# One gather tile in 64 of a graph layer's second loop: fetched row by row on SyncE instead of gathered on GpSimd

## The chip, the cores and the metric

One core of one Trainium2 chip. The metric is the device time of one execution in microseconds. The runs of the kernel before took 2174.53, 2178.26 and 2182.04 us; the median is 2178.26 us.

## What is computed

Two layers of a graph network, on 6,250 nodes (128 numbers each) and 106,250 edges that are sorted by receiving node. The first layer is finished when the stretch of this case begins. The second layer, cut to what matters:

```python
src, dst = edge_index
msg_in = concat([x[src], x[dst]], axis=1)            # 106250 x 256
for t in range(4):                                    # four edge types
    h = relu(msg_in @ W1[t] + b1[t]);  m = h @ W2[t] + b2[t]
    score = sigmoid(msg_in @ attn_w[t] + attn_b[t])
    msgs += where(edge_type == t, m * score, 0)
agg = zeros.at[dst].add(msgs)
x = layernorm(layernorm(gru(agg, x) + x) * gamma + beta + x)   # per node
```

`x[src] @ W1` does not depend on the edge but on the pair (node, type). The kernel therefore makes a table of it first, `p_tab` in DRAM, with one row of 129 f32 numbers (516 bytes) for each node and type: 128 for the hidden layer and one for the score. For each edge one row of that table has to be fetched, by a row number that is data.

## The kernel before, in words

Two loops over the edges stand one behind the other, one for each layer; the change lies in the second (function `edges1`). Edges are cut into tiles of 128 (one edge on each partition), 8 tiles make a step (`TPS`), and 4 steps make a loop (`SLOTS`), one for each slot of the ring buffer `gp[:, slot, tile, :]`. There are 104 steps (`STEPS`) in 26 loops (`LOOPS`), 831 tiles in all, since the last step has 7.

**GpSimd (POOL)** does the gathers. `gather_step` (L636) issues one indirect DMA for each tile (L639): it takes 128 row numbers from the index tile `idx` and fetches 128 rows of `p_tab` into `gp`. `gather_loop` (L645) runs the steps: before each it waits for the index tile (`idx_in`), for the slot to be free (`used`, one count for each step whose rows were added by VectorE), and from loop `LEAD_LONG` = 6 on for `paced` (`e_mm`, TensorE's count of finished groups), which holds GpSimd back to at most two steps ahead of TensorE.

**VectorE (DVE)**, in `edge_rows` (L2175), waits for a slot's gathers (`landed[u]`, 16 for each tile) and adds the gathered rows to TensorE's receiver rows: three additions for a step (L2187). It then frees the slot (`used`), adds sums into the accumulators (L2164, L2167) and makes one-hot matrices (L2142 to L2150). **ScalarE (ACT)** applies sigmoid and relu (L1886, L1890), and its queue also issues the index tiles (`load_idx`, L1762), the receivers' windows (`load_windows`, L1754, four DMAs for a step whose row numbers are loaded into registers by `run_starts`, L632 and L633) and the key rows (`load_row`). **TensorE (PE)** multiplies the windows by one-hot matrices (L2005) and sums the messages (L2094).

Behind the edges run the nodes, in units of 256: unit g = i - 3 is worked on in loop i, a piece in each of the four steps. Its transfers are all that **SyncE (SP)** does in this stretch, in the loop at L1840: wait for `xt_used`, load `x_t` (L1824, read by TensorE in `node_gates`, first at L2028, and by VectorE); wait for `y_ok` in `store` (L1829) and write the previous unit's rows to `out` (L1831, waited for in VectorE's `new_rows`, L2305); wait for `xr_used` and load the rows `x_row` (L1827). The order on each engine's queue is written out by hand, and all waits are on semaphores.

Of the kernel before, what the change touches and what calls it, by code (L numbers as in the profile page):

```python
# [23 lines left out]
P = 128  # L24
# [38 lines left out]
N_LATER = 29  # L63
FULL = -(-E // P) - (STEPS - 1) * TPS
FIRST_PART = 4
KEY_AT = 2 * TPS * P + PPS
ROWS = -(-(STEPS + 2) // 16) * 16

# [48 lines left out]
def build(nc, a, out):  # L117

    top = ExitStack()
    with top:  # L120
# [22 lines left out]
            x1=nc.dram_tensor("x1_d", [NP, H], f32).ap(),  # L143
            x1_t=nc.dram_tensor("x1_t_d", [P, CHUNKS * CH * P], f32).ap(),
            p_tab=nc.dram_tensor("p_tab_d", [NP * T, PW], f32).ap(),
            q_tab=nc.dram_tensor("q_tab_d", [CHUNKS * CH * P * T, PW], f32).ap(),
        )
        later = update_weights(nc, m)
# [493 lines left out]
        ).then_inc(landed[h], 16)  # L642


def gather_loop(e, idx, idx_in, table, buf, landed, used, gate, last_landed, paced, rate):  # L645


    slots = len(landed)

    def steps(start, stop, pace):  # L650
        with e.Fori(start, stop) as i:  # L651
            for h in range(slots):
                e.wait_ge(idx_in[h], i * 16 + 16)
                e.sem_inc(gate, 1)
                e.wait_ge(used, i * slots + (h + 1))  # L655
                e.sem_inc(gate, 1)  # L656
                if pace:
                    e.wait_ge(paced, i * (slots * rate) + rate * (h + 1 - LEAD))  # L658
                    e.sem_inc(gate, 1)
                gather_step(e, idx, table, buf, landed, h)  # L660

    steps(1, LEAD_LONG, False)
    steps(LEAD_LONG, LOOPS - 1, True)
    for h in range(slots):
        e.wait_ge(idx_in[h], (LOOPS - 1) * 16 + 16)
        e.sem_inc(gate, 1)
        e.wait_ge(used, (LOOPS - 1) * slots + (h + 1))
        e.sem_inc(gate, 1)
        e.wait_ge(paced, rate * ((LOOPS - 1) * slots + (h + 1 - LEAD)))
        e.sem_inc(gate, 1)  # L670
        if h < slots - 1:
            gather_step(e, idx, table, buf, landed, h)
    gather_step(e, idx, table, buf, landed, slots - 1, range(FIRST_PART))
    gather_step(e, idx, table, buf, dict([(slots - 1, last_landed)]), slots - 1, range(FIRST_PART, FULL))

# [995 lines left out]
def edges1(nc, k, dram, later, nodes, out, left):  # L1671


    with ExitStack() as ctx:
# [16 lines left out]
        ps_s = ps_row[:, 0:2 * PPS * WIN].rearrange("p (h g w) -> p h g w", h=2, g=PPS)  # L1691
        iota, part = ps_row[:, 2 * PPS * WIN:2 * PPS * WIN + P], ps_row[:, 3 * P:3 * P + 1]
        landed = m.sems("landed1", SLOTS)
        win_in, row_in = m.sems("win_in", 2), m.sems("row_in", 2)
        gate = gate_v = k["gate"]
        (used, hot_ok, hx_ok, e_mm, pre_ok, score_ok, hid_ok, sc_ok, sum_mm, acc_own, score_own, zero_ok) = (
# [49 lines left out]
        def own_count(g, z):  # L1746
            return 0 if z is last_rest else g

        def own_f_count(g, z):
            return own_count(g, z) * OWN_F - (1 if z is first_rest else 0)  # L1750

        with nc.Block(no_gpsimd_drain=True) as block:

# [12 lines left out]
            def _(e):  # L1766
# [70 lines left out]
                load_x_t(0, UN, usual)  # L1837
                e.wait_ge(xr_used, 1)
                load_x_row(0, UN, usual)
                with e.Fori(1, UNITS) as g:  # L1840
                    e.wait_ge(xt_used, g + 1)
                    load_x_t(g, UN, usual)
                    store(g - 1, UN, usual)
                    e.wait_ge(xr_used, g + 1)
                    load_x_row(g, UN, usual)
                for (g, n), z, u in zip(REST, (first_rest, last_rest), (1, 0)):
                    e.wait_ge(used, SLOTS + STEPS - SLOTS + u + 1)
                    e.wait_ge(xt_ld, 16 * g)
                    load_x_t(g, n, z)
# [12 lines left out]
            @block.gpsimd  # L1862
            def _(e):
                for u in range(SLOTS):
                    e.wait_ge(idx_in[u], 16)
                    e.sem_inc(gate, 1)
                    gather_step(e, idx, dram["p_tab"], gp, landed, u)
                gather_loop(e, idx, idx_in, dram["p_tab"], gp, landed, used, gate, landed[SLOTS - 1], e_mm, NQ)

                def root(g, n, c, z):  # L1870
                    mine = rstd[:, z["at"]:z["at"] + n // P]
                    e.wait_ge(z["var_ok"], own_count(g, z) * 2 + (c + 1))
                    e.tensor_tensor(mine, mine, minus_half[:, 0:n // P], ALU.pow).then_inc(z["root_ok"], 1)

                for c in range(2):
                    root(UNITS - 1, UN, c, before_rest)
                left.run(e, "gpsimd", left.flag(e, "gpsimd"))

            @block.scalar
            def _(e):  # L1880
# [54 lines left out]
                def steps(i, unit, before, first=False, last=False, table=False):  # L1935
                    for u in range(SLOTS):
                        j, h = i * SLOTS + u, u % 2
                        if not last and not first:
                            e.wait_ge(landed[u], i * (16 * TPS) + 16 * TPS)
                            load_idx(e, j + SLOTS, u)  # L1940
                        if table:
                            table_out(j + (AHEAD - 1), CH - 1)
# [196 lines left out]
            def _(e):  # L2139
# [32 lines left out]
                    some = slice(lo * CH, hi * CH)  # L2172
                    e.memset(first_buf[:, some, :], 0.0).then_inc(zero_ok, 1)

                def edge_rows(i, u, before, clear=False, final=False):  # L2175


                    j, h = i * SLOTS + u, u % 2
# [1 line left out]
                    if gone:  # L2180
                        e.memset(gp[:, u, FULL:TPS, :], 0.0).then_inc(iota_ok, 1)
                        e.wait_ge(iota_ok, 3)
                    e.wait_ge(landed[u], i * (16 * TPS) + 16 * (FULL if gone else TPS))
                    for q, mine in enumerate(groups):
                        n = mine.stop - mine.start
                        e.wait_ge(e_mm, j * NQ + (q + 1))
# [142 lines left out]
                def steps(i, first, unit, before, last=False):  # L2329
                    for u in range(SLOTS):  # L2330
                        if last and u == SLOTS - 1:
                            adds(STEPS - 2, 0)
                        edge_rows(i, u, not first or u > 0, first and u == 1, last)
                        if first and u == 0:
                            clear_first(0, CH)
                        if before and u == 0:
# [124 lines left out]
```

## Time and profile before

| what | value |
|---|---|
| runs of the kernel before | 2174.53, 2178.26, 2182.04 us |
| the profiled execution's own time | 2180.23 us |
| its span in the trace | 2178.1 us |
| second loop's gathers, first start to last start | 1107.63 to 2149.43 us |
| granted TensorE clock, mean of the span | 0.895 |

Times in the trace count from the first instruction. A queue's name with a q behind it (SPq, ACTq, POOLq) is the engine's own instruction stream: DMA issues, register arithmetic and semaphore instructions stand there and are not counted as busy. FUSED_REGOPS, ALU_OP and MOVE are register arithmetic, TENSOR_LOAD reads registers from memory. The duration of a DMA instruction is what its issue takes on the engine; the time until its data is there is called landing.

### The profile page before, as it was taken

How to read it: one execution, taken by the hardware profiler on the slowest of the kernel's cores; microseconds unless marked ns; L12 is line 12 of the kernel's file. 1: busy time of each engine (PE TensorE's matmuls, PEld its weight loads, DVE VectorE, ACT ScalarE, POOL GpSimd, SP SyncE). 2: the span in 40 equal slices, each digit the busy share in tenths (PEclk: the TensorE clock that was granted, in tenths of full speed). 3: DMA queues.
4: the chain of work that ended last, by engine and by line, in shares of the span. 5: the costliest groups of instructions: out<-in, count | busy, mean ns of one | idle time of the engine just before them, and what ended most of it. 6: DMA issues, size and time to landing. Idle time of an engine off the chain costs nothing. (4 is left out here: it accounts for less than half of the span.)

```text
span 2178.1 us, 43658 instructions
## 1 busy us (share of the span) xinstructions
PE 1773.3 (81%) x9981; PEld 1422.8 (65%) x9981; DVE 1470.1 (67%) x3717; ACT 1334.7 (61%) x4373; POOL 1606.5 (74%) x1698
## 2 busy tenths in 40 slices
PE   6897999999999999999877876766766666677767
PEld 3675766676666666666646775666666666666666
DVE  6657655555655555555557687777777777777877
ACT  6676877777877877777535544544554454544444
POOL 6777777777777777777657777777777777777773
PEclk7898999999999999999989988888887988887888
DMA  8422233232322322322368855454444445444452
GB/s 287 126 56 59 75 83 80 73 87 75 83 78 75 84 77 76 82 78 75 83 177 231 225 122 122 109 117 117 115 117 112 117 113 119 110 119 116 110 124 53
DMA packets 220027, 236.10 MB, mean 108 GB/s; under 512 B 72844, under 2 KB 162744, under 8 KB 219547
## 3 DMA queue, kind: packets, MB, share of 16 engines
q0 software_dynamic: 53744, 112.66, 22.1%
q10 hardware_dynamic: 87968, 56.13, 10.2%
q1 hardware_dynamic: 78267, 66.78, 9.9%
q8 instruction: 16, 0.26, 0.0%
q14 instruction: 32, 0.26, 0.0%
HBM read 190.83 MB, written 44.57 MB: 108 GB/s over the span
## 5 line engine op out<-in xcount | busy, mean ns | idle before, releaser
L639 POOL DMA_INDIRECT gp<-p_tab_d,idx x831 | 789.6, 950 | 277.7 <-issue 247.9
L639 POOL DMA_INDIRECT gx<-node_d,idx x831 | 800.2, 963 | 262.4 <-issue 235.7
L729 ACT ACTIVATE msg<-ws,y 128x32 f32<-128x32 f32 x2448 | 539.9, 309 | 86.2 <-DVE ws L705 85.8
L1000 PEld LDWEIGHTS ps_a<-hot,msg 128*128 128x128 f32 x3324 | 412.0, 199 | 209.0 <-DVE msg L714 106.5
L2005 PE MATMUL ps_e<-win,hot_x 128*128 128x129 f32 x1664 | 303.0, 356 | 266.2 <-DVE hid L2187 243.6
L1000 PE MATMUL ps_a<-hot,msg 128*128 128x128 f32 x3324 | 435.0, 286 | 75.8 <-DVE msg L714 53.5
L2005 PEld LDWEIGHTS ps_e<-win,hot_x 128*128 128x128 f32 x1664 | 278.5, 261 | 288.8 <-DVE hid L2187 250.8
L708 DVE TENSOR_TENSOR vy<-gx,y 128x768 f32<-128x768 f32 (+1 forms) x105 | 99.6, 948 | 307.6 <-DMA gx<-node_d,idx 307.5
L1890 ACT ACTIVATE hid<-hid,score 128x128 f32<-128x128 f32 x832 | 277.9, 393 | 10.1
L2187 DVE TENSOR_TENSOR hid<-ps_e,gp 128x387 f32<-128x387 f32 (+1 forms) x312 | 141.7, 509 | 143.2 <-DMA gp<-p_tab_d,idx 139.3
L1886 ACT ACTIVATE score<-hid 128x3 f32<-128x3 f32 (+1 forms) x312 | 61.0, 195 | 272.5 <-DVE hid L2187 267.8
L687 PE MATMUL ps_w<-w,h 128*128 128x256 f32 x832 | 223.4, 415 | 0.0
L2094 PEld LDWEIGHTS ps_g<-hot,hid 128*128 128x128 f32 x1664 | 212.1, 200 | 6.4 <-ACT hid L1890 0.3
L2094 PE MATMUL ps_g<-hot,hid 128*128 128x128 f32 x1664 | 212.0, 282 | 0.1
L687 PEld LDWEIGHTS ps_w<-w,h 128*128 128x128 f32 x832 | 159.3, 202 | 67.9 <-issue 48.3
L190 ACT ACTIVATE h<-ps_h,b 128x512 f32<-128x512 f32 x208 | 141.3, 679 | 85.2 <-PE ps_h L195 81.6
L2142 DVE TENSOR_TENSOR hot_x<-key_row,ps_s 128x1024 f32<-128x1024 bf16 x104 | 126.0, 1212 | 32.8 <-PE ps_s L2100 27.5
L2164 DVE TENSOR_TENSOR acc<-acc,ps_g 128x128 f32 x416 | 119.5, 287 | 14.4 <-issue 2.1
L1140 DVE TENSOR_TENSOR hot<-ps_a,dloc 128x1024 f32<-128x1024 f32 x104 | 126.6, 1217 | 0.0
L2150 DVE TENSOR_TENSOR hot<-ps_s,key 128x1024 f32<-128x1024 f32 x104 | 126.4, 1215 | 0.0
L996 PE MATMUL ps_h<-emb,w 16*128 16x512 f32 x202 | 113.2, 640 | 2.4 <-DMA emb<-emb_d 2.4
L195 PE MATMUL ps_h<-h,w 128*128 128x512 f32 x208 | 110.1, 611 | 0.7 <-ACT h L190 0.7
(295 smaller groups left out, 2155.2 us busy)
## 6 DMA issues: line engine op xcount, KB each, us to landing
win<-q_tab_d ACTq DMA_DIRECT2D x408, 64.5 KB
key_row<-key_row_d ACTq DMA_DIRECT2D x100, 256.0 KB, 3.9
gx<-node_d,idx POOLq DMA_INDIRECT x831, 2.7
gp<-p_tab_d,idx POOLq DMA_INDIRECT x831
p_tab_d<-acc SPq DMA_DIRECT2D x23, 516.0 KB
q_tab_d<-unit_area SPq DMA_DIRECT2D x36, 258.0 KB, 3.9
q_tab_d<-acc SPq DMA_DIRECT2D x5, 774.0 KB, 5.3
emb<-emb_d SPq DMA_DIRECT2D x102, 32.0 KB
```

The costliest lines, as they stand in the source:

```text
L190: e.activation(mlp[f"h{layer}"][:], mlp["ps_h"][:], ACT.Silu, bias=w[f"b{layer - 1}"][:]).then_inc(ok, 1)
L639: e.indirect_dma_start(out=buf[:, h, t, :], out_offset=None, in_=table, in_offset=bass.IndirectOffsetOnAxis(ap=idx[:, h, t:t + 1], axis=0) ...
L687: last = e.matmul(ps_w[:, 2 * t:2 * t + 2, :], h2[:, t * P:(t + 1) * P], w["w2"][:], start=False, stop=t % 2 == 1)
L729: last = e.activation(self.cols[1][:, tile, c, :], self.ws[:, tile, :], ACT.Copy, scale=y[:, c:c + 1])
L1000: last = e.matmul(ps_a[:, h, b, :], msgs[h].tile(t, b), hot[:, h, t, :], start=t == tiles.start, stop=t == tiles.stop - 1)
L1140: e.tensor_tensor(hot[:, h], spread(ps_a[:, h, IOTA, :], 1, TPS), spread(w["dloc"][:, bass.ds(j * TPS, TPS)], 2, P), ALU.is_equal)
L1890: last = e.activation(hid[:, h, t, 0:H], hid[:, h, t, 0:H], ACT.Relu, scale=score[:, h, t:t + 1])
L2005: last = e.matmul(ps_e[:, q, at:at + PW], hot_x[:, h, t, :], win[:, h, t // 2, :], start=True, stop=True)
L2094: e.matmul(ps_g[:, h, t // 2, :], hid[:, h, t, 0:H], hot[:, h, t, :], start=t % 2 == 0, stop=t % 2 == 1)
L2142: e.tensor_tensor(hot_x[:, h].rearrange("p t n -> p (t n)"), key_row[:, h, :], part.to_broadcast([P, TPS * P]), ALU.is_equal).then_inc(hx_ ...
L2150: e.tensor_tensor(hot[:, h], spread(iota[:, 0:P], 1, TPS), spread(k["key"][:, tiles], 2, P), ALU.is_equal).then_inc(hot_ok, 1)
L2187: e.tensor_tensor(hid[:, h, mine, :], ps_e[:, q, 0:n * PW].rearrange("p (t n) -> p t n", t=n), gp[:, u, mine, :], ALU.add).then_inc(pre_ok, 1)
```

## The change

The last tile of the last slot (slot 3, tile 7) is taken from GpSimd in every second loop from loop 6 on: loops 6, 8, ..., 24, which makes `FAR_TILES` = 10 tiles of the 831. In those loops GpSimd gathers 31 tiles and in the others 32, so its loop is written with two rounds in the body.

SyncE fetches these tiles. At its start it copies the ten columns of row numbers from `p_idx` into `far_idx` in DRAM with one DMA (10 x 128 numbers of 4 bytes, both sides non-contiguous). For each tile it loads the tile's 128 row numbers into one partition of `far_i`; then it loads 16 of them at a time into registers and issues 16 DMAs, each of one row of `p_tab` (516 bytes) into one partition of the side buffer `far[:, b, :]`, which has two halves and lies in the unused constant `zero`. Of the 128 rows 64 are issued in each of two loops: 48 between the load of `x_t` and the store, and 16 behind the load of `x_row`. When all 128 have landed (`far_ld`) and the ring's slot is free (`used`), one DMA copies the half into `gp[:, 3, 7, :]`.

The waits change with it: VectorE and ScalarE wait in slot 3 for a count of `landed` that leaves the moved tiles out (`last_landed`, register arithmetic on the loop's number), VectorE also for the copy (`far_ok`); a `sem_inc` of the unused count `gate` stands behind each of these waits, in ScalarE in all four slots.

```diff
 FIRST_PART = 4
+FAR_TILES = (LOOPS - LEAD_LONG) // 2
+FAR_REGS = 16
+FAR_EARLY = 48
 KEY_AT = 2 * TPS * P + PPS
...
             p_tab=nc.dram_tensor("p_tab_d", [NP * T, PW], f32).ap(),
+            far_idx=nc.dram_tensor("far_idx_d", [FAR_TILES, P], u32).ap(),
             q_tab=nc.dram_tensor("q_tab_d", [CHUNKS * CH * P * T, PW], f32).ap(),
...
 
-def gather_loop(e, idx, idx_in, table, buf, landed, used, gate, last_landed, paced, rate):
+def gather_loop(e, idx, idx_in, table, buf, landed, used, gate, last_landed, paced, rate, far=False):
 
...
 
-    def steps(start, stop, pace):
-        with e.Fori(start, stop) as i:
-            for h in range(slots):
-                e.wait_ge(idx_in[h], i * 16 + 16)
+    def round_of(i, pace, tiles=TPS):
+        for h in range(slots):
+            e.wait_ge(idx_in[h], i * 16 + 16)
+            e.sem_inc(gate, 1)
+            e.wait_ge(used, i * slots + (h + 1))
+            e.sem_inc(gate, 1)
+            if pace:
+                e.wait_ge(paced, i * (slots * rate) + rate * (h + 1 - LEAD))
                 e.sem_inc(gate, 1)
-                e.wait_ge(used, i * slots + (h + 1))
-                e.sem_inc(gate, 1)
-                if pace:
-                    e.wait_ge(paced, i * (slots * rate) + rate * (h + 1 - LEAD))
-                    e.sem_inc(gate, 1)
-                gather_step(e, idx, table, buf, landed, h)
-
-    steps(1, LEAD_LONG, False)
-    steps(LEAD_LONG, LOOPS - 1, True)
+            gather_step(e, idx, table, buf, landed, h, range(tiles if h == slots - 1 else TPS))
+
+    with e.Fori(1, LEAD_LONG) as i:
+        round_of(i, False)
+    if far:
+        with e.Fori(0, FAR_TILES - 1) as q:
+            round_of(q * 2 + LEAD_LONG, True, TPS - 1)
+            round_of(q * 2 + (LEAD_LONG + 1), True)
+        round_of(LEAD_LONG + 2 * (FAR_TILES - 1), True, TPS - 1)
+    else:
+        with e.Fori(LEAD_LONG, LOOPS - 1) as i:
+            round_of(i, True)
     for h in range(slots):
...
         landed = m.sems("landed1", SLOTS)
+        far = k["zero"][:, 0:2 * PW].rearrange("p (b f) -> p b f", b=2)
+        far_i = k["zero"][0:1, 2 * PW:2 * PW + P].bitcast(u32)
+        far_in, far_ok, far_ld = m.sem("far_in"), m.sem("far_ok"), m.sems("far_ld", 2)
         win_in, row_in = m.sems("win_in", 2), m.sems("row_in", 2)
...
 
+        def last_landed(i, n=TPS):
+            if isinstance(i, int):
+                return i * (16 * TPS) + 16 * n - 16 * max(0, (i - (LEAD_LONG - 2)) // 2)
+            pair = (i - (LEAD_LONG - 2)) // 2
+            return pair * (16 * (2 * TPS - 1)) + (i % 2) * (16 * TPS) + 16 * TPS * (LEAD_LONG - 1)
+
+        def far_count(i):
+            if isinstance(i, int):
+                return 16 * max(0, (i - (LEAD_LONG - 2)) // 2) + 32
+            return (i - (LEAD_LONG - 2)) // 2 * 16 + 32
+
         with nc.Block(no_gpsimd_drain=True) as block:
...
                 load_x_row(0, UN, usual)
-                with e.Fori(1, UNITS) as g:
+                first_far = (LEAD_LONG + 1) * SLOTS * TPS - 1
+                far_cols = dram["p_idx"][:, first_far:first_far + (FAR_TILES - 1) * 2 * SLOTS * TPS + 1:2 * SLOTS * TPS]
+                e.dma_start(dram["far_idx"].rearrange("q p -> p q"), far_cols, allow_slow_non_contiguous=True)\
+                    .then_inc(far_in, 16)
+                e.wait_ge(far_in, 16)
+                e.sem_inc(far_ok, 32)
+                far_regs = [e.alloc_register(f"far{n}") for n in range(FAR_REGS)]
+
+                def far_rows(b, lo, hi):
+                    for at in range(lo, hi, FAR_REGS):
+                        e.load(far_regs, far_i[:, at:at + FAR_REGS])
+                        for n, r in enumerate(far_regs):
+                            row = e.snap(r, min_val=0, max_val=NP * T - 1)
+                            e.dma_start(far[at + n:at + n + 1, b, :], dram["p_tab"][bass.ds(row, 1), :])\
+                                .then_inc(far_ld[b], 16)
+
+                def unit_io(g, rows=None):
                     e.wait_ge(xt_used, g + 1)
                     load_x_t(g, UN, usual)
+                    if rows is not None:
+                        b, lo = rows
+                        far_rows(b, lo, lo + FAR_EARLY)
                     store(g - 1, UN, usual)
...
                     load_x_row(g, UN, usual)
+                    if rows is not None:
+                        far_rows(b, lo + FAR_EARLY, lo + P // 2)
+
+                with e.Fori(0, FAR_TILES // 2) as n:
+                    for b in range(2):
+                        at, g = n * 4 + (2 * b + LEAD_LONG), n * 4 + (2 * b + 1)
+                        e.dma_start(far_i, dram["far_idx"][bass.ds(n * 2 + b, 1), :]).then_inc(far_in, 16)
+                        e.wait_ge(far_ok, n * 32 + (16 * b + 16))
+                        e.sem_inc(gate, 1)
+                        e.wait_ge(far_in, n * 32 + (16 * b + 32))
+                        e.sem_inc(gate, 1)
+                        unit_io(g, (b, 0))
+                        unit_io(g + 1, (b, P // 2))
+                        e.wait_ge(far_ld[b], n * (16 * P) + 16 * P)
+                        e.sem_inc(gate, 1)
+                        e.wait_ge(used, at * SLOTS + SLOTS)
+                        e.sem_inc(gate, 1)
+                        e.dma_start(gp[:, SLOTS - 1, TPS - 1, :], far[:, b, :]).then_inc(far_ok, 16)
+                with e.Fori(2 * FAR_TILES + 1, UNITS) as g:
+                    unit_io(g)
                 for (g, n), z, u in zip(REST, (first_rest, last_rest), (1, 0)):
...
                     gather_step(e, idx, dram["p_tab"], gp, landed, u)
-                gather_loop(e, idx, idx_in, dram["p_tab"], gp, landed, used, gate, landed[SLOTS - 1], e_mm, NQ)
+                gather_loop(e, idx, idx_in, dram["p_tab"], gp, landed, used, gate, landed[SLOTS - 1], e_mm, NQ, far=True)
 
...
                         if not last and not first:
-                            e.wait_ge(landed[u], i * (16 * TPS) + 16 * TPS)
+                            if u == SLOTS - 1 and unit:
+                                e.wait_ge(landed[u], last_landed(i))
+                            else:
+                                e.wait_ge(landed[u], i * (16 * TPS) + 16 * TPS)
+                            e.sem_inc(gate, 1)
                             load_idx(e, j + SLOTS, u)
...
 
-                def edge_rows(i, u, before, clear=False, final=False):
+                def edge_rows(i, u, unit, before, clear=False, final=False):
 
...
                         e.wait_ge(iota_ok, 3)
-                    e.wait_ge(landed[u], i * (16 * TPS) + 16 * (FULL if gone else TPS))
+                    if u == SLOTS - 1 and unit:
+                        e.wait_ge(landed[u], last_landed(i, FULL if gone else TPS))
+                        e.sem_inc(gate, 1)
+                        e.wait_ge(far_ok, far_count(i))
+                        e.sem_inc(gate, 1)
+                    else:
+                        e.wait_ge(landed[u], i * (16 * TPS) + 16 * TPS)
                     for q, mine in enumerate(groups):
...
                             adds(STEPS - 2, 0)
-                        edge_rows(i, u, not first or u > 0, first and u == 1, last)
+                        edge_rows(i, u, unit, not first or u > 0, first and u == 1, last)
                         if first and u == 0:
```

## Rows read from the trace of the kernel before

**Rows 1.** Page, part 1, busy time of the engines over the whole span.

```profile
PE 1773.3 (81%) x9981; PEld 1422.8 (65%) x9981; DVE 1470.1 (67%) x3717; ACT 1334.7 (61%) x4373; POOL 1606.5 (74%) x1698
```

**Rows 2.** Page, part 4, the chain that ended last, shares by engine.

```profile
POOL 30%; issue 13%; PE 2%; DMA 2%; DVE 1%; POOLq 0%; ACT 0%; DVEq 0%
```

**Rows 3.** Page, part 5, gathers of the second loop: busy, mean ns, idle.

```profile
L639 POOL DMA_INDIRECT gp<-p_tab_d,idx x831 | 789.6, 950 | 277.7 <-issue 247.9
```

**Rows 4.** Who waited for whom, POOL, 1100 to 2178 us.

```profile
POOL gp L639 <- issue: 247.9, 813, 0.3
POOL gp L639 <- PE ps_e L2005: 4.6, 15, 0.3
```

**Rows 5.** Timeline of POOL: first and last of the 831 gathers.

```profile
1107.63 0.94 POOL L639 DMA_INDIRECT gp<-p_tab_d,idx  x1 [24.58 <-POOLq L783]
...
2149.43 0.94 POOL L639 DMA_INDIRECT gp<-p_tab_d,idx  x1 [0.30 <-issue]
```

**Rows 6.** Timeline of one loop: two of SP's transfers, PE's use of x_t.

```profile
1710.66 0.40 SPq L1831 DMA_DIRECT2D out<-unit_area  x1
...
1719.05 0.34 SPq L1824 DMA_DIRECT2D unit_area<-x_t_d  x1
...
1734.74 0.60 PE L2028 MATMUL ps_v<-unit_area,w_ih 128*128 128x256 f32 x2
...
1759.35 0.34 SPq L1824 DMA_DIRECT2D unit_area<-x_t_d  x1
```

**Rows 7.** Stretch 1400 to 2100 us: busy time, clock, DMA share, GB/s.

```profile
1400.00:2100.00 700.00, 489.57 (x2930) 454.86 (x2931) 544.91 (x1637) 341.43 (x944) 530.16 (x558) 0.83 0.49 115
```

**Rows 8.** Timeline of DVE, the step's first addition, slots 2, 3, 0.

```profile
1701.93 1.36 DVE L2187 TENSOR_TENSOR hid<-ps_e,gp 128x387 f32<-128x387 f32 x3 [0.52 <-DMA gp<-p_tab_d,idx]
...
1711.94 1.36 DVE L2187 TENSOR_TENSOR hid<-ps_e,gp 128x387 f32<-128x387 f32 x3 [1.47 <-DMA gp<-p_tab_d,idx]
...
1722.46 1.36 DVE L2187 TENSOR_TENSOR hid<-ps_e,gp 128x387 f32<-128x387 f32 x3 [2.71 <-DMA gp<-p_tab_d,idx]
```

**Rows 9.** Line L1756 (window DMAs with row numbers in registers), by operation.

```profile
L1756 ACTq MOVE win<-q_tab_d x408: 29/29/29, 1143.0 to 2138.6; - x136
L1756 ACTq DMA_DIRECT2D win<-q_tab_d x408: 339/340/1064, 1143.1 to 2138.7; - x136
L1756 ACTq FUSED_REGOPS  x306: 46/46/57, 1143.5 to 2138.5; - x153
```

**Rows 10.** Timeline: four such DMAs in a row on ACT.

```profile
1705.73 1.86 ACTq L1756 DMA_DIRECT2D win<-q_tab_d  x4
```

**Rows 11.** Line L264, small loads of 4 rows and of 3 rows.

```profile
L264 SPq DMA_DIRECT2D b<-in_b x4: 297/330/413, 83.0 to 84.1; - x4
L264 SPq DMA_DIRECT2D att_b<-in_attn_b x1: 276/276/276, 78.1 to 78.1; - x1
```

**Rows 12.** Timeline: four loads of 4 rows each, one after another, on SP.

```profile
82.99 1.50 SPq L264 DMA_DIRECT2D b<-in_b  x4
```

**Rows 13.** Lines L1145 (one register loaded), L632 (four) and L633 (their snaps).

```profile
L1145 DVEq TENSOR_LOAD <-start x105: 302/308/1019, 71.8 to 1095.3; - x105
...
L632 DVEq TENSOR_LOAD <-start x104: 339/344/362, 1151.4 to 2159.8; - x104
L632 ACTq TENSOR_LOAD <-start x102: 303/308/729, 1142.5 to 2136.6; - x102
...
L633 ACTq FUSED_REGOPS  x102: 163/163/170, 1142.8 to 2136.9; - x102
```

**Rows 14.** Lines L1824 and L1831, transfers of 128 KB: issue to landing.

```profile
DMA to landing us min/median/max: 1.8/3.1/3.4
...
DMA to landing us min/median/max: 1.7/2.1/2.6
```

**Rows 15.** Page, part 3, queues that fetch instructions: packets, MB, share.

```profile
q8 instruction: 16, 0.26, 0.0%
q14 instruction: 32, 0.26, 0.0%
```

## The prediction, made before the changed kernel ran

> **What bounds the kernel now.** The page comes first. Over the whole span POOL is busy 74%, less than PE's 81% and little more than DVE's 67% [rows 1]; by these shares nothing would be decided. But they mix two loops and the work around them, and the chain that ended last is made of POOL for 30% and of "issue" for 13%, against 2% for PE and 1% for DVE [rows 2]. The costliest group says what that is: 831 gathers of 950 ns, with 0.3 us of idle time in front of each that ends with no release, only with the next issue [rows 3]. So one gather costs POOL 1.25 us from start to start whatever else happens. The list of waits from 1100 us on confirms it: 813 gaps of at most 0.3 us have no release, 15 of the same length are put down to PE, and there is no longer one in the loop [rows 4]. The first gather starts at 1107.63 us and the last at 2149.43 us: 1041.80 us over 830 intervals are 1.2552 us for each [rows 5]. The loop is 831 gathers long and nothing else. A loop of 32 tiles takes 40.17 us, and SP's timeline has that rhythm too: its loads of x_t start at 1719.05 and 1759.35 us [rows 6].
>
> The engines behind POOL have room. From 1400 to 2100 us DVE is busy 545 of 700 us, PE 490 and ACT 341 [rows 7]. DVE's first addition of a step waits for the gathers' landing every time: 0.52 us in slot 2, 1.47 in slot 3, 2.71 in slot 0 [rows 8].
>
> **The change, part by part.** The removed part: ten gathers less on POOL, 10 x 1.2552 = 12.6 us, all on the path that sets the end, since the last moved tile (loop 24) lies before the last gather and the tail behind it stays as it is. POOL's extra register arithmetic for the unrolled rounds costs nothing: its stream runs ahead of gathers of 1.25 us, and every gap is 0.3 us in the loop that has such arithmetic today [rows 4]. If that cover failed, a step's few operations of 0.03 to 0.06 us would show as longer gaps.
>
> What follows in the far step: slot 3's gathers are issued in 8.76 instead of 10.04 us, so they land 1.26 us earlier against DVE's work. DVE's idle time there is 1.47 us [rows 8], less some ten added queue operations (arithmetic of `last_landed` and `far_count`, two counts, one more wait), at the 46 ns of a FUSED_REGOPS [rows 9] about 0.4 us. DVE may be 0.2 us late in ten steps; the next slot has 2.71 us of room, and POOL does not notice, as it waits for `used` and `paced` only of steps it passed long ago. Cost: nothing; without that room, 10 x 0.2 = 2 us at most. ScalarE's added counts (four in a loop) and its own arithmetic lie beside its idle half [rows 7].
>
> The added part is SP's, and the question is whether SP gets 128 rows, 8 register loads and its old work done within two loops, 2 x 40.17 - 1.26 = 79.1 us. There is no such one-row DMA in the trace. Its nearest relatives:
> - With row numbers in registers, ACT issues four window DMAs in 1.86 us; one takes 0.34 us, so from start to start it is (1.86 - 0.34) / 3 = 0.507 us [rows 10], of which 0.340 is the DMA and 0.167 the MOVE, the FUSED_REGOPS and the gaps [rows 9]. These have 128 rows.
> - Loads of 4 rows or 3 rows take 276 to 330 ns, one 413 [rows 11], and four of them in a row 1.50 us, 0.375 each with a gap [rows 12]. I take 0.30 us for the DMA itself.
> - Each row is also snapped; four snaps and the first address take ACT 163 ns [rows 13], so about 0.035 us for one if it is merged into the address operation.
> I take 0.30 + 0.167 + 0.035 = 0.50 us for a row. Below, 0.276 + 0.121 = 0.40 (no gap lengthened); above, 0.507 + 0.046 = 0.553 (the row costs what the 128-row DMA costs, and its snap is an operation of its own).
> - Loading one register takes DVE 308 ns, four 344; ACT loads four in 308 [rows 13]. The slope is 12 ns a register: 16 cost 0.31 + 12 x 0.012 = 0.45 us, with a gap 0.50. Upper end by rows: each register for itself, 4.9 us.
> - Six old transfers at 0.47 us: 2.8 us. The copy and the fetch of row numbers 0.9 us; two waits for landing (row numbers, last rows), as a 128 KB transfer lands in 2.1 us [rows 14], 4.2 us.
> - SP's loop body has some 800 instructions, and its backward jump may wait for code. The whole run shows 48 packets of instruction fetch [rows 15], so before most loops never fetch; I put 0 to 3.4 us (the longest landing of rows 14) on each pass of four loops, and take 1 us for two loops.
>
> Sum for two loops: 128 x 0.50 = 64.3 (with 0.502), 8 x 0.50 = 4.0, 2.8, 0.9, 4.2 and 1.0: 77.2 of 79.1 us. It fits, with 2 us to spare. The order fits as well: 48 rows take 24 us and three loads 1.5, so they end 26 us behind the load of x_t, while the store's release comes 31.8 us behind it (1710.66 + 40.17 - 1719.05) [rows 6]; the last 16 rows then run about 1 us into the next x_t, and the end of a pair makes that about 6 us. PE needs x_t 15.7 us behind its load (1734.74 - 1719.05) [rows 6], of which landing takes 3.4 at most [rows 14]: 12.3 us may be lost before anybody waits. The finished side buffer is due one loop behind its copy, 40 us, and costs nothing. The DMA that collects the ten columns runs once, in front of SP's loop; if it takes long, it spends some of these 12.3 us once.
>
> SP's rows also load the DMA engines. 128 rows of 516 bytes replace 128 gathered rows, and the copy moves them once more; at a share of 0.49 [rows 7] that delays a landing by some tenths at most, not POOL's issue.
>
> On register loads the rows and a rule differ. The Trainium skill, page "Runtime: NRT & Kernel Launch", section "Instruction fetch mechanics", says that a register load costs about 200 ns a register even in bulk; it speaks of loads from HBM, ours read SBUF, and the 12 ns a register above speak against it here. By the page 16 registers would take 3.2 us and SP 99.2 us for two loops. That is a rival below, and its time is worked out there from rows.
>
> The sum: the profiled execution took 2180.23 us (span 2178.1), 2 us above the median of the runs. 2180.2 - 12.6 = 2167.7 us for it, 2178.3 - 12.6 = 2165.7 us against the median. I forecast **2166 us**.
>
> **The rivals.**
> A. The forecast: POOL stays the bound. Chance 0.61.
> B. SP becomes the bound, and the kernel gets slower. Its place is PE's wait for x_t in `node_gates`; behind it stand the receivers' products of the next step, so DVE, and through `paced` POOL. It decides from the point where two loops on SP exceed 79.1 us by more than 12.3/10 us, that is from 0.527 us for a row. At 0.553 us SP needs 128 x 0.553 + 12.9 = 83.7 us; 10 x 4.6 - 12.3 = 34 us are lost, 12.6 won: 2178 + 21 = 2199 us. For it: one-row DMAs may cost as much as large ones, and ACT's 0.507 us [rows 10] is close to the limit. Against: the small loads' 0.28 to 0.33 us [rows 11]. Chance 0.20.
> C. Registers load one after the other: by rows, 16 x 0.308 = 4.9 us instead of 0.45, SP 77.2 + 8 x 4.48 = 113 us for two loops, 10 x 33.9 - 12.3 - 12.6 = 314 us more: 2492 us. The Trainium skill's 200 ns would give 2178 + 10 x 20.1 - 24.9 = 2354 us (an estimate from the page named above). The 12 ns a register speak against both. Chance 0.04.
> D. Half-way: SP late by just as much as was won, a row at 0.53 to 0.542 us, or a code fetch at each jump at its upper end: between 2170 and 2185 us. Chance 0.13.
> E. The gathers' issue slows down because SP's row stream keeps DMA engines busy. Against: over the whole loop, with all the transfers it has today, the mean is 1.2552 us and no gap is long [rows 4, 5]. Chance 0.02, about 2180 us.
>
> **How the numbers follow.** About 0.3%, 6.5 us, is what a measurement of this kernel can tell from no change. Faster by more than that is A and little else: 0.62. Within it lie most of D and E: 0.13. Slower: B, C and the rest of D: 0.25. The range runs from 2161 us (the sum, less the 4 us by which the fastest run before lay under its median) to 2200 us, which takes in D and B's worked case and leaves C and the worse half of B out.
>
> **What would show it.** Right: 821 gathers on POOL, still 1.25 us apart with gaps of 0.3 us, the last starting near 2137 us; on SP one-row DMAs 0.50 us apart, register loads under 0.5 us, the store issued within 1 us of its release; DVE's idle time in slot 3 of far steps near 0.2 us and still ended by a landing. Wrong: PE L2028 waiting for unit_area<-x_t_d, or POOL gaps ended by PE L2005 that exceed 0.3 us (B); TENSOR_LOAD of some microseconds (C); idle time of SP in front of the DMA behind a jump (D); a mean gather above 1.26 us (E).

## The result, and the profile after

The changed kernel takes 2290.66 us (median of 5 runs, 2283.91 to 2292.39), the kernel before beside it 2182.04 us: ratio 1.0496, 95% interval 1.0481 to 1.0511, 108.6 us slower. Beside e1 to e4 below the kernel before itself took 2842 us and beside e5 to e7 2812 us, and the traces of those seven kernels have added gaps of about 3 us in front of 33 to 48 gathers, so that mainly the durations of single instructions are read from them, and the runs that decide stand beside a kernel before of 2176 to 2180 us.

Page of the changed kernel, part 1; it answers to [rows 1].

```profile
PE 1778.8 (78%) x9981; PEld 1420.0 (62%) x9981; DVE 1469.4 (64%) x3717; ACT 1330.5 (58%) x4373; POOL 1600.8 (70%) x1688
```

POOL's busy time is 5.7 us less, and the other engines' is what it was; nothing in the row says why the span grew by 108.6 us. Part 4 of the same page does (the chain that ended last, by engine and then by line), where [rows 2] had POOL 30%:

```profile
SPq 31%; issue 10%; DMA 3%; PE 2%; DVE 2%; POOL 1%; ACT 1%; ACTq 1%; DVEq 0%; POOLq 0%
SPq L1878 14%; SPq L1875 12%; SPq L1877 2%; POOL gp L643 1%; DMA win<-q_tab_d 1%; PE ps_e L2073 1%; DMA zero<-p_tab_d 1%; DMA zero<-far_idx_d 1%; DMA q_tab_d<-unit_area 1%; ACT hid L1954 1%; ACTq L1781 0%; SPq L1852 0%; SPq L1856 0%; PE ps_g L2162 0%; SPq L1849 0%
```

SP's instruction stream is now the chain: L1878 is the one-row DMA, L1875 the load of 16 registers, and L1877 the snap. Part 5 (busy, mean ns of one, idle before), beside [rows 3]:

```profile
L643 POOL DMA_INDIRECT gp<-p_tab_d,idx x821 | 781.1, 951 | 383.3 <-issue 236.2
L2096 PE MATMUL ps_v<-unit_area,w_ih 128*128 128x256 f32 x96 | 49.3, 613 | 153.6 <-DMA unit_area<-x_t_d 153.6
```

A gather is what it was, 951 ns, and there are ten less. The idle time in front of them grew from 277.7 to 383.3 us. The second row is new among the costliest groups: TensorE waits 153.6 us for x_t, the load of SP that stands behind the rows. Who waited for whom, POOL's waits first (us in total, times, longest), beside [rows 4], then the other engines' from 1350 to 2250 us:

```profile
POOL gp L643 <- issue: 236.2, 772, 0.6
POOL gp L643 <- PE ps_e L2073: 120.1, 42, 10.7
```

```profile
PE ps_v L2096 <- DMA unit_area<-x_t_d: 153.6, 19, 12.4
DVE unit_area L2382 <- DMA out<-unit_area: 81.8, 18, 5.8
```

POOL is held back by `paced` in 42 places, up to 10.7 us long, where before the 15 gaps put down to PE were 0.3 us each. 120.1 - 42 x 0.3 = 107.5 us were lost so. TensorE waits 19 times for x_t, about 8 us each, and VectorE's wait at L2382 for the store of `out` (another of SP's transfers) is new too. Timeline of POOL, first and last gather, beside [rows 5]:

```profile
1112.32 0.95 POOL L643 DMA_INDIRECT gp<-p_tab_d,idx  x1 [25.27 <-POOLq L794]
```

```profile
2250.31 1.15 POOL L643 DMA_INDIRECT gp<-p_tab_d,idx  x1 [0.30 <-issue]
```

The loop of gathers lasts 1137.99 us from first start to last start instead of 1041.80: 96.2 us more, and 107.5 - 12.6 = 95 is that. Another 7.7 us lie behind the last gather (36.4 us to the end of the span instead of 28.7), where the node units' last pieces come late. Together these are 103.9 us. The remaining 4.7 us of the spans' difference of 108.6 lie before the first gather (1112.32 against 1107.63) and are hardly the change's: with the same change in place the first gather starts at 1102.1 us in e12, 1105.3 in e9 and 1112.1 in e8.

Now SP itself, in one round of two loops, beside [rows 6]. L1896 fetches a tile's row numbers, L1849 loads x_t, L1878 are the rows, L1856 the store, L1852 the load of x_row, L1907 the copy into the ring:

```profile
1377.46 0.55 SPq L1907 DMA_DIRECT2D gp<-zero  x1
1378.23 0.26 SPq L1896 DMA_DIRECT2D zero<-far_idx_d  x1
1379.87 0.36 SPq L1849 DMA_DIRECT2D unit_area<-x_t_d  x1
1383.95 27.58 SPq L1878 DMA_DIRECT2D zero<-p_tab_d  x48
1411.62 0.43 SPq L1856 DMA_DIRECT2D out<-unit_area  x1
1412.26 0.40 SPq L1852 DMA_DIRECT2D unit_area<-x_d  x1
1416.35 6.91 SPq L1878 DMA_DIRECT2D zero<-p_tab_d  x16
1423.52 0.37 SPq L1849 DMA_DIRECT2D unit_area<-x_t_d  x1
...
1460.22 6.60 SPq L1878 DMA_DIRECT2D zero<-p_tab_d  x16
1468.63 0.51 SPq L1907 DMA_DIRECT2D gp<-zero  x1
1472.88 0.25 SPq L1896 DMA_DIRECT2D zero<-far_idx_d  x1
1474.81 0.37 SPq L1849 DMA_DIRECT2D unit_area<-x_t_d  x1
```

From one fetch of row numbers to the next it is 1472.88 - 1378.23 = 94.65 us here, and over the eight intervals between 1378.2 and 2118.9 us 92.6 us on average. POOL needs 79.1. SP has no idle stretch to speak of: x_t is loaded the moment the rows in front of it are out, and behind each transfer there is a gap of 3.7 us before the next row, for instance from 1412.66 to 1416.35. That gap is the register load:

```profile
L1875 SPq TENSOR_LOAD <-zero x80: 3460/3532/3747, 1290.1 to 2197.6; - x80
```

3.53 us for 16 registers, against 0.31 for four in [rows 13]. SP itself has two such short loads of four registers in the changed kernel's trace, from the tensor `start` (L636 there):

```profile
L636 SPq TENSOR_LOAD <-start x2: 300/316/332, 1125.4 to 1133.8; - x2
```

The rows themselves are cheap (snap and address, then MOVE and DMA), beside [rows 9]:

```profile
L1877 SPq FUSED_REGOPS  x1280: 44/44/56, 1293.6 to 2207.7; - x183
...
L1878 SPq MOVE zero<-p_tab_d x1280: 29/29/37, 1293.7 to 2207.7; - x183
L1878 SPq DMA_DIRECT2D zero<-p_tab_d x1280: 217/228/299, 1293.8 to 2207.8; - x183
```

A one-row DMA is issued in 228 ns, not in 300 or 340, and 16 rows take 6.60 us from first start to last end (at 1460.22 us above), (6.60 - 0.23) / 15 = 0.42 us each.

### The profile page after: what moved, and what is told of

It reads as the page before. It is cut to its first block, busy times and chain, and to the rows that moved or that the text cites. A ratio compares the mean times of both kernels' runs of the same rounds, so it can differ in the third digit from the quotient of the medians.

```text
span 2286.7 us, 47811 instructions
## 1 busy us (share of the span) xinstructions
PE 1778.8 (78%) x9981; PEld 1420.0 (62%) x9981; DVE 1469.4 (64%) x3717; ACT 1330.5 (58%) x4373; POOL 1600.8 (70%) x1688
## 4 chain that ended last, share of the span: by engine, by line
SPq 31%; issue 10%; DMA 3%; PE 2%; DVE 2%; POOL 1%; ACT 1%; ACTq 1%; DVEq 0%; POOLq 0%
SPq L1878 14%; SPq L1875 12%; SPq L1877 2%; POOL gp L643 1%; DMA win<-q_tab_d 1%; PE ps_e L2073 1%; DMA zero<-p_tab_d 1%; DMA zero<-far_idx_d 1%; DMA q_tab_d<-unit_area 1%; ACT hid L1954 1%; ACTq L1781 0%; SPq L1852 0%; SPq L1856 0%; PE ps_g L2162 0%; SPq L1849 0%
## 5 line engine op out<-in xcount | busy, mean ns | idle before, releaser
L643 POOL DMA_INDIRECT gp<-p_tab_d,idx x821 | 781.1, 951 | 383.3 <-issue 236.2
L2073 PE MATMUL ps_e<-win,hot_x 128*128 128x129 f32 x1664 | 282.0, 339 | 198.3 <-DVE hid L2261 172.3
L2073 PEld LDWEIGHTS ps_e<-win,hot_x 128*128 128x128 f32 x1664 | 260.8, 246 | 216.8 <-DVE hid L2261 178.5
L2162 PEld LDWEIGHTS ps_g<-hot,hid 128*128 128x128 f32 x1664 | 219.3, 206 | 10.6 <-issue 3.4
L2162 PE MATMUL ps_g<-hot,hid 128*128 128x128 f32 x1664 | 218.6, 288 | 2.9 <-ACT hid L1954 2.6
L2096 PE MATMUL ps_v<-unit_area,w_ih 128*128 128x256 f32 x96 | 49.3, 613 | 153.6 <-DMA unit_area<-x_t_d 153.6
L1965 ACT ACTIVATE unit_area<-ps_v,b_rz 128x256 f32<-128x256 f32 x48 | 20.2, 471 | 234.7 <-PE ps_v L2097 227.8
L2096 PEld LDWEIGHTS ps_v<-unit_area,w_ih 128*128 128x128 f32 x96 | 25.7, 296 | 162.6 <-DMA unit_area<-x_t_d 158.9
```

Source lines behind the costliest of these rows:

```text
L643: e.indirect_dma_start(out=buf[:, h, t, :], out_offset=None, in_=table, in_offset=bass.IndirectOffsetOnAxis(ap=idx[:, h, t:t + 1], axis=0) ...
L2073: last = e.matmul(ps_e[:, q, at:at + PW], hot_x[:, h, t, :], win[:, h, t // 2, :], start=True, stop=True)
L2162: e.matmul(ps_g[:, h, t // 2, :], hid[:, h, t, 0:H], hot[:, h, t, :], start=t % 2 == 0, stop=t % 2 == 1)
```

## The experiments

The first idea was that loads of many registers are long and loads of four are short, since [rows 13] had four for 0.31 us. All kernels differ from the changed one by the lines shown.

**e1: four registers a load.**

```diff
-FAR_REGS = 16
+FAR_REGS = 4
```

> Rows are loaded 4 registers at a time instead of 16 (32 loads for a tile instead of 8). Theory L (the long register loads are the cause: 16 registers take 3.53 us, while 4 took 0.31 us before): 32 loads of 0.31 to 0.35 us and a gap are 13 us for two loops instead of 29, SP needs about 76 us and fits into 79.1; POOL is the bound again and the time is the kernel before's less 12.6 us, 2169 us against 2182. Rival R (the 128 row DMAs and the waits for landing are the cause, whatever the loads): the time stays at 2290 us. Rival S (a register costs 0.22 us wherever it is loaded): 128 registers remain 28 us, 2290 us as well, and a load of 4 lasts 0.9 us.

**e2: eight registers a load.**

```diff
-FAR_REGS = 16
+FAR_REGS = 8
```

> Rows are loaded 8 registers at a time. Theory L has two forms. If every register beyond the fourth costs about 0.27 us ((3.53 - 0.31) / 12), a load of 8 takes 1.4 us, 16 of them 24 us with gaps, SP needs 86 us for two loops: 10 x 7 - 12 - 12.6 = 45 us slower, about 2228 us. If a load above some length changes its kind and costs 0.22 us for each register, 8 take 1.8 us: 16 x 1.9 = 30 us, and the time is that of 16 registers, 2290 us. If 8 are still short (0.35 us), 2169 us. Rival R: 2290 us with any length of load.

Measured beside a kernel before of 2842 us: e1 3198.8 us (ratio 1.126), e2 3158.1 us (1.112). Four registers are worse than eight. The load's line in e1, and in the same run the short loads of the kernel before (L636 there), which answer to [rows 13]; then e2:

```profile
L1875 SPq TENSOR_LOAD <-zero x320: 3/1122/1287, 1727.0 to 3108.5; - x160
```

```profile
L636 ACTq TENSOR_LOAD <-start x102: 18/308/789, 1514.5 to 3155.2; - x102
L636 SPq TENSOR_LOAD <-start x2: 334/521/708, 1467.6 to 1482.9; - x2
```

```profile
L1875 SPq TENSOR_LOAD <-zero x160: 16/1922/2032, 1719.7 to 3050.8; - x160
```

Theory L falls in its simple form. A load of four takes 1.12 us here and 0.31 us on ACT in the same run, so neither the number of registers nor the longer times of these runs make it long. The engine does not either: SP's own loads of `start` took 0.32 us in the changed kernel. 1.12, 1.92 and 3.53 us for 4, 8 and 16 registers are 0.3 us and 0.2 us for each register: rival S was nearly right for these loads, and the loads of `start` are of another kind. What differs: `start` is read at multiples of 16 bytes from its beginning, the row numbers lie at column 258 of the constant, byte 1032 from its beginning, which is a multiple of 8 only; and `start` is read as int32, they as uint32.

**e3: one load for a tile.**

```diff
                     for at in range(lo, hi, FAR_REGS):
-                        e.load(far_regs, far_i[:, at:at + FAR_REGS])
+                        if at == 0:
+                            e.load(far_regs, far_i[:, at:at + FAR_REGS])
```

> Leaves out: registers are loaded once for a tile (16 of them), and the 128 row DMAs use these 16 row numbers again and again; the moved tiles' values are not the reference's. The number, size and issue of the row DMAs stay. Theory L: SP loses 7 x 3.6 = 25 us for two loops, needs 66 us, POOL is the bound: 2169 us against 2182. Rival R (row DMAs): 2290 us. A mixture would give a time between.

**e4: no loads and no rows.**

```diff
                     for at in range(lo, hi, FAR_REGS):
-                        e.load(far_regs, far_i[:, at:at + FAR_REGS])
-                        for n, r in enumerate(far_regs):
-                            row = e.snap(r, min_val=0, max_val=NP * T - 1)
-                            e.dma_start(far[at + n:at + n + 1, b, :], dram["p_tab"][bass.ds(row, 1), :])\
-                                .then_inc(far_ld[b], 16)
+                        e.sem_inc(far_ld[b], 16 * FAR_REGS)
```

> Leaves out: no register loads and no row DMAs, SP only counts them as done; the copy into the ring, all waits and the register arithmetic of DVE, ACT and POOL stay. It is the ceiling of the idea: both theories expect ten gathers less on POOL, 10 x 1.2552 = 12.6 us, 2169 us against 2182. If DVE's or ACT's added queue work costs something, it shows here as a time above 2171 us with POOL gaps longer than 0.3 us.

e3 came to 2992.9 us (ratio 1.052) and e4 to 2825.3 us (0.993). Neither tells what bounds the changed kernel at 2290 us, as the timeline of POOL in e4 shows:

```profile
2006.08 0.95 POOL L643 DMA_INDIRECT gp<-p_tab_d,idx  x1 [2.83 <-PE ps_e L2069]
...
2018.74 0.94 POOL L643 DMA_INDIRECT gp<-p_tab_d,idx  x1 [2.98 <-remote]
```

A gather waits 2.8 or 3.0 us here although SP does nothing but transfers. The sums of the prediction hold for a POOL that never waits, so these two were run again later (e9 and e11).

**e5 and e6: the row numbers at a multiple of 64 bytes; e6 with four registers a load.**

```diff
-        far_i = k["zero"][0:1, 2 * PW:2 * PW + P].bitcast(u32)
+        far_i = k["zero"][0:1, 384:384 + P].bitcast(u32)
```

> Only the place of the 128 row numbers changes: column 384 of the constant (byte 1536, a multiple of 64) instead of column 258 (byte 1032, a multiple of 8 only). The loads of the kernel before, 4 registers in 0.31 us, all begin at multiples of 16 bytes; the changed kernel's never do, and took 0.22 us for each register. Theory A (the address decides): a load of 16 aligned registers takes 0.3 to 0.5 us instead of 3.53, SP needs 128 x 0.42 + 8 x 0.5 + 8 = 66 us of 79.1 for two loops, POOL is the bound, and the time is 12.6 us under the kernel before (2169 against 2182; ratio 0.994). Rival C (a register of this kind of load costs 0.2 us wherever it lies): load 3.5 us, ratio 1.05 as in the changed kernel. Rival N (the number decides: up to 4 registers are short): the same as C for 16.

> The same place (column 384) and 4 registers a load. In the unaligned place a load of 4 took 1.12 us. Theory A: 0.31 us; 32 loads with gaps are 13 us for two loops, SP needs 75 us of 79.1, ratio 0.994. Rival C: 1.12 us, SP needs 128 x 0.42 + 32 x 1.2 + 8 = 100 us for two loops, ratio 1.08 to 1.10. It tells theory A from the rival that only loads with more than 4 registers are long: that one expects 1.12 us here too, since the unaligned 4 were long.

**e7: the old place, read as int32.**

```diff
-                        e.load(far_regs, far_i[:, at:at + FAR_REGS])
+                        e.load(far_regs, far_i[:, at:at + FAR_REGS].bitcast(i32))
```

> The old place (column 258), 16 registers, but read as int32 like the short loads of the kernel before instead of as uint32. Theory A: nothing changes, 3.5 us a load, ratio 1.05. Rival T (the type decides): short loads, ratio 0.994.

The load's line in e5, e6 and e7:

```profile
L1875 SPq TENSOR_LOAD <-zero x80: 5/1158/1362, 1709.4 to 2881.3; - x80
```

```profile
L1875 SPq TENSOR_LOAD <-zero x320: 2/554/1379, 1718.1 to 2953.5; - x160
```

```profile
L1875 SPq TENSOR_LOAD <-zero x80: 1312/3461/3639, 1713.6 to 2956.8; - x80
```

The place decides: 16 registers take 1.16 us instead of 3.53, four 0.55 instead of 1.12. The type changes nothing (3.46 us): rival T is out, and so are rival C and rival N. But theory A named 0.3 to 0.5 us for 16 and 0.31 for four, and that was too low. The times (2976.1, 3030.5 and 3054.4 us, where the kernel before took 2812) say nothing of the loss of 108.6 us, for the reason given above.

They do say where the idea ends. With the short loads in place e5 is still 5.8% slower than the kernel before beside it (ratio 1.0577), and e3, with one load a tile, 5.2%, while e4, without rows and loads, is not slower (0.993). One of e5's blocks of 48 rows:

```profile
2019.91 45.88 SPq L1878 DMA_DIRECT2D zero<-p_tab_d  x48
```

It takes twice the 23 us that it takes in e8 below, and in e5 TensorE waits for x_t 16 times again, 124.8 us in total. There SP's row stream is too long for its two loops even with the right address. So what follows holds for executions of about 2.17 ms.

**e8: e5 once more.**

> The kernel with the row numbers at column 384 and 16 registers a load once more, since the kernel before itself took 2.81 ms in the call that ran it first, with gaps of some microseconds on every engine, and there the bound was not POOL's pace. A load of 16 aligned registers took 1.16 us. Where the kernel before takes 2182 us: SP needs 128 x 0.42 + 8 x 1.26 + 8 = 72 us of 79.1 for two loops, POOL is the bound, 2182 - 12.6 = 2169 us, ratio 0.994 (theory A). Rival R (beside the loads something else keeps SP or the ring late): between 2169 and 2290 us, with PE waiting for x_t at L2096.

2168.91 us (2166.59 to 2171.36) against 2179.62 us for the kernel before: ratio 0.9951, interval 0.9939 to 0.9963. **Only the place of 128 numbers in SBUF was changed, and the change goes from 5% slower to 0.5% faster.** Its load, POOL's waits, and one round of two loops on SP:

```profile
L1875 SPq TENSOR_LOAD <-zero x80: 1156/1215/1438, 1293.2 to 2065.1; - x80
```

```profile
POOL gp L643 <- issue: 240.3, 788, 0.3
POOL gp L643 <- PE ps_e L2073: 4.9, 16, 0.3
```

```profile
1683.17 0.36 SPq L1849 DMA_DIRECT2D unit_area<-x_t_d  x1
1684.94 23.12 SPq L1878 DMA_DIRECT2D zero<-p_tab_d  x48
1708.98 0.43 SPq L1856 DMA_DIRECT2D out<-unit_area  x1
1711.41 6.91 SPq L1878 DMA_DIRECT2D zero<-p_tab_d  x16
...
1759.48 0.50 SPq L1907 DMA_DIRECT2D gp<-zero  x1
1762.73 0.25 SPq L1896 DMA_DIRECT2D zero<-far_idx_d  x1
```

POOL has no gap between gathers over 0.3 us any more. 48 rows with two loads between them take 23 us instead of 27.5, and the store at 1708.98 us follows them after 0.9 us of waiting. From 1200 to 2200 us SP waits for VectorE's result in 17 places:

```profile
SPq L1856 <- DVE unit_area L2354: 99.5, 17, 28.6
```

Two of these waits, 55.8 us, lie behind the last row (after 2078 us), as the changed kernel's only two do (41.0 us, after 2210 us). The other 15, 43.7 us in total, lie between the rows, where the changed kernel's SP has none: SP is not the bound here.

**e9: e4 once more, the ceiling.**

> Leaves out: register loads and row DMAs; SP counts them as done and copies what the side buffer holds. Everything else of the change stays (ten gathers less on POOL, the copies, the waits, the arithmetic on DVE, ACT and POOL). The aligned kernel came out 10.7 us under the kernel before, the sum says 12.6. If SP's row stream costs POOL or the landings nothing (theory A), this has the same time as the aligned kernel within 2 us: ratio 0.994 to 0.995. If the row stream costs something (rival E of the prediction), this is faster than that by more than 2 us: ratio under 0.993.

2165.59 against 2176.12 us, ratio 0.9954 (0.9940 to 0.9967). SP's 1280 row DMAs and 80 loads, all of them left out here, cost nothing that can be measured in e8 (0.9951, 0.9939 to 0.9963). The traces say it more closely: from the first start to the last the gathers take 1027.2 us here and 1027.7 us in e8.

**e10: e1 once more (column 258, four registers).**

> Row numbers at column 258 (byte 1032), 4 registers a load. Theory A (an address that is no multiple of 16 bytes makes every register cost 0.2 us): a load of 4 takes 1.12 us, 32 of them with gaps 39 us; SP needs 54 + 39 + 8 = 101 us of 79.1 for two loops: 10 x 22 - 12.3 - 12.6 = 195 us slower, 2377 us, ratio 1.09, worse than with 16 registers. The number-of-registers theory (4 registers short as in the kernel before): 0.31 us, ratio 0.994.

```profile
L1875 SPq TENSOR_LOAD <-zero x320: 1031/1123/1245, 1288.6 to 2296.4; - x160
```

```profile
POOL gp L643 <- PE ps_e L2073: 218.1, 54, 13.8
```

2378.73 against 2176.12 us, ratio 1.0929 (1.0912 to 1.0945): theory A's 2377. POOL now waits for PE in 54 places, up to 13.8 us long. The same rows, the same gathers and the same number of registers in smaller loads make the kernel slower still than the changed one, by some 90 us.

**e11: e3 once more (column 258, one load a tile).**

> Leaves out: at column 258, registers are loaded once for each tile instead of eight times, and the 128 row DMAs use these 16 numbers again, so the moved tiles hold other rows. All row DMAs stay. Theory A: 7 x 3.6 = 25 us less on SP for two loops, 66 us of 79.1: POOL is the bound, 2169 us, ratio 0.994 to 0.995. Rival R (the row DMAs and landings): as the changed kernel, ratio 1.05.

```profile
L1876 SPq TENSOR_LOAD <-zero x10: 3476/3484/3502, 1291.9 to 1993.5; - x10
```

2165.22 us, ratio 0.9947 (0.9931 to 0.9962). The load is as long as ever, there are 10 of them instead of 80, and the loss is gone with all row DMAs in place: rival R is out for these executions.

**e12: column 260, byte 1040, a multiple of 16 but not of 32.**

```diff
-        far_i = k["zero"][0:1, 2 * PW:2 * PW + P].bitcast(u32)
+        far_i = k["zero"][0:1, 260:260 + P].bitcast(u32)
```

> Row numbers at column 260: byte 1040, a multiple of 16 but not of 32 or 64. If 16 bytes are the unit, a load of 16 registers takes 1.16 us as at column 384 and the time is 2169 us; if it is 64 bytes, 3.5 us and 2290 us.

```profile
L1875 SPq TENSOR_LOAD <-zero x80: 1158/1224/1402, 1280.5 to 2055.1; - x80
```

1.22 us a load, and 2160.16 us in its one run. A multiple of 16 bytes is enough: a move by two columns, 8 bytes, takes 2.3 us off each load. Of the other addresses only those 8 bytes past a multiple of 16 were tried.

## Why the prediction was wrong

The bound of the kernel before, and what the change takes away. Right. e9 gives 10.5 us for ten gathers less and e8 10.7, where 12.6 were forecast, and e8's loop of gathers lasts 2139.85 - 1112.1 = 1027.7 us instead of 1041.8. The forecast of 2166 us is what e8, e9 and e11 measured (2168.91, 2165.59 and 2165.22); the kernel that was changed did not get there.

**The step that failed** is the term for the register loads, "The slope is 12 ns a register: 16 cost 0.31 + 12 x 0.012 = 0.45 us, with a gap 0.50." Measured: 3.53 us, with a gap 3.6. Eight times 3.1 us are 25 us too little in SP's two loops. The slope was read from loads of one and four registers whose addresses are multiples of 16 bytes, and was carried to loads whose address is not; the change's own line `2 * PW` with `PW` = 129 says so, and the prediction did not look at it. The term's upper end (4.9 us) held the value, but was kept out of the range by the weight given to the slope. The Trainium skill, page "Runtime: NRT & Kernel Launch", section "Instruction fetch mechanics", gives about 200 ns a register even in bulk. By that rule a load costs 3.2 us, and these loads agree: 0.2 us a register at 4, 8 and 16. The loads at multiples of 16 bytes do not: (1.16 - 0.55) / 12 = 0.05 us a register, and 0.31 us for four of `start`. Rival C was this mechanism, a price for each register, and was given 4%. Its load (4.9 us) and its rows (0.50 us) were both too dear, so the 2290 us lie below its 2492 and above rival B's 2199, at the place that B had named.

The other terms of SP's sum, two loops each. Rows: 128 x 0.42 = 53.8 us, not 64.3, since a DMA with one row is issued in 228 ns and not in 300; the nearest relatives (0.28 to 0.41 us) were all dearer. The six old transfers take 0.37 to 0.43 us of issue each, the copy 0.5 and the fetch 0.26; with register arithmetic and gaps that is the 3.7 us put down. Waits for landing, 4.2 forecast, the changed kernel's, in the stretch from 1300 to 2250 us:

```profile
SPq L1904 <- DMA zero<-p_tab_d: 12.5, 10, 1.6
SPq L1900 <- DMA zero<-far_idx_d: 9.7, 9, 1.5
```

(12.5 + 9.7) / 10 = 2.2 us. The backward jump, forecast at 0 to 3.4 us a pass: behind the copy at 1377.46 us the next fetch follows after 0.22 us, behind the one at 1468.63 us, where the loop's jump lies, after 3.74 us; at the other three jumps it is 2.97, 2.73 and 3.77 us, 3.3 us on average and 1.7 us for two loops. The instruction queue shows the code that is fetched again, first in the changed kernel, beside [rows 15], then in e9:

```profile
q14 instruction: 71, 0.58, 0.1%
```

```profile
q14 instruction: 34, 0.27, 0.0%
```

These are 39 packets more than before, and all but two of them go with the rows' code: in e9, whose loop has none of it, the gap at the jump is about 0.5 us (behind the copies at 1428.71 and 1586.58 us). A sentence of the same section of the Trainium skill says that a taken branch to a page outside the window waits for its fetch, and the trace agrees. The sum with measured terms: 53.8 + 8 x 3.63 + 3.7 + 2.2 + 1.7 = 90.4 us, and 92.6 were measured.

From there on the prediction's arithmetic held, in total, to some 7 us. 10 x (92.6 - 79.1) - 12.3 - 12.6 = 110 us; measured 108.6, but that this is so close is in part luck. The sum has 123 us lost by POOL, and the trace has 107.5; it has nothing for the tail, which lost 7.7; and 4.7 us of the measured difference of the spans lie before the first gather. For e10 the same sum gave 195 us and 202.6 came. The place was right too: TensorE's wait for x_t, then VectorE, then POOL through `paced`. Only the condition "from 0.527 us for a row" was put in the row's terms, while the load exceeded it.

VectorE in the far step: right in the argument. In e8 the first additions of slots 2, 3 and 0 around a moved tile, beside [rows 8]:

```profile
1690.65 1.36 DVE L2261 TENSOR_TENSOR hid<-ps_e,gp 128x387 f32<-128x387 f32 x3 [2.13 <-DMA gp<-p_tab_d,idx]
...
1700.28 1.36 DVE L2261 TENSOR_TENSOR hid<-ps_e,gp 128x387 f32<-128x387 f32 x3
...
1710.33 1.36 DVE L2261 TENSOR_TENSOR hid<-ps_e,gp 128x387 f32<-128x387 f32 x3 [1.38 <-DMA gp<-p_tab_d,idx]
```

In slot 3 (1700.28) the idle time is gone, as the argument had it ("DVE may be 0.2 us late"); the list of signs, with idle time near 0.2 us, did not fit that argument. (Seven gathers take 8.79 us, not 8.76; nothing hangs on it.) In slot 0 there are 1.38 us again (0.35 behind the next moved tile, at 1788.58 us), and POOL does not see it. Rival E is out by e9: 1027.7 us of gathers with the row stream, 1027.2 without. Rival D did not come about.

## What to carry to other kernels

Price an operation by the form that the change issues, address and size included, and where the trace shows only a friendlier form, keep the dear end in the range: here 0.31 and 3.53 us were the same instruction. When work is moved to an idle queue, write that queue's time for one period beside the bound's period (77 of 79 us was no margin for terms known to a factor of ten), and look for the old transfer that stands behind the new work, since its reader is the first to wait. Put numbers that are loaded into registers at multiples of 16 bytes. And see what the queue's margin is in executions that are slow for other reasons: here the same kernel is 0.5% faster (e8) or 5.8% slower (e5).

## What was not expected of the hardware

In these runs a load of registers from SBUF took 0.3 us and 0.2 us for each register where its address was a multiple of 8 bytes only (1.12, 1.92 and 3.53 us for 4, 8 and 16 registers in e10, e2 and the changed kernel), and 1.16 to 1.22 us for 16 at multiples of 16 bytes (1536 in e5 and e8, 1040 in e12). Why four aligned ones took 0.55 us in e6 and four of `start` 0.32 us on the same engine was not tried, nor why the address matters. A DMA of one row of 516 bytes was issued in 228 ns, one of 128 rows in 340 [rows 9]. And 1280 such one-row DMAs beside POOL's gathers did not move the gathers' pace: 1.253 us on average in e8, and the same in e9 without them.
